# The gated stage of a one-core decoder kernel: another order of loads, four banks for turned rows, and a tile of their own for the narrow unit's weights

## The chip, the cores and the metric

The kernel runs on one core of a Trainium2 chip. The metric is the device time of one execution in microseconds. A core has TensorE (PE, products; PEld is its weight load), VectorE (DVE), ScalarE (ACT), GpSimd (POOL), and SyncE (SP), which in this kernel issues nearly all DMAs. Each engine runs its own list of instructions in order and waits on semaphores.

## The reference

Two gated cross-attention layers and two gated feed-forward layers act on x (16 batches of 128 tokens of 1024 features). The change lies in the last of them, a SwiGLU with low-rank additions to its weights:

```python
def _matmul_lora(x, w, a, b, scale=1.0):
    out = jnp.einsum('bsd,hd->bsh', x, w)
    out = out + jnp.einsum('bsr,hr->bsh', jnp.einsum('bsd,rd->bsr', x, a), b) * scale
    return out
gate = _matmul_lora(x, gate_w, gate_a, gate_b)      # hidden size 2752, rank 16
up = _matmul_lora(x, up_w, up_a, up_b)
hidden = jax.nn.silu(gate) * up
out = _matmul_lora(hidden, down_w, down_a, down_b)
# in the model, with x normalised along its last axis:
x = x + jnp.tanh(g_ffn[1]) * _L1_ffn_ref(_layernorm(x, axis=-1), ...)
```

## The kernel before

The stage before this one (`lane_attention`) normalises its results and stores them in DRAM as x3n, in seven forms of 512 columns for each token (halves and sums of halves). The gated stage (`swiglu_ffn`) computes gate and up for 128 hidden units at a time by a seven-product scheme on 2x2 blocks, in place of eight products. There are 22 such units of weights (NF), the last with 64 hidden columns (`narrow`), and two passes over them, one for each half of the tokens: NU = 44 units in all, LAST = 21. Each product is three matmuls (high and low parts) for each of four column blocks.

**Turned rows.** The token operand of each of the seven products needs four "rows" (128 tokens x 512 columns of x3n), so 28 rows for each pass. SyncE loads a row into one of five places (`row`, L1980: two halves of the third weight tile raw[2], two of lb, one of its own), TensorE turns it into a PSUM bank (`turn`, L2704, counted by xt), ScalarE casts the high part (`high_x`, xh), VectorE subtracts for the low part (`low_x`, xl). Rows 0 to 27 are turned while unit 0's products run, four during each product, one ahead of each column block (`three`, L2747). Rows 28 to 47 are turned during the narrow unit 21, rows 48 to 55 during the first two products of unit 22, which starts the second pass. `turned(n)` says which bank a row is turned into; a turn waits until the row two before it is evacuated. The wait `x_there` at the head of a product lets it start only when all rows of its operand are in place.

**Weights.** In the first pass the raw weights of a unit (gate and up, 512 KB each) are loaded into raw[0] and raw[1] (unit 1: into `second`). TensorE forms their low-rank addition from small factors (`merge`), VectorE adds it in place (`add`, wa), forms four sums (`first_sums`, `second_sums`), ScalarE casts high parts (`high`, `high_sum`, wh), GpSimd subtracts for low parts (`low`, wl). The merged weights are stored in DRAM (`store_merged`) and loaded from there in the second pass. `load_raw(u)` waits until the previous contents are used up (wl) and stored (mst). The narrow unit's 64 + 64 columns are loaded into raw[0].

**Orders.** SyncE's list is written out by hand (L2155 to L2250), and so are ScalarE's (L2391 on) and VectorE's (L2614 on). VectorE's order in one unit is first_and_sixth, gate_even, add, with_seventh, add, first_sums, with_fifth, second_sums, up_even, hidden_even, gate_odd, hidden_odd. The last token row of the first half isn't normalised before the stage begins: VectorE takes its statistics (`last_statistics`), GpSimd the power -0.5, VectorE the normalised row (`last_row`, yn), GpSimd four forms (`row_sums`, tr), and SyncE stores them to x3n. Eight PSUM banks: six go round among the products (`bank`), 6 and 7 serve merges.

## Time and profile before

| | us |
|---|---|
| median of 3 runs | 3319.41 (3316.63 to 3323.08) |
| profiled execution | 3314.45 |
| its span | 3312.5 |
| mean granted clock of TensorE | 0.974 |

The span runs from the first to the last instruction of the one profiled execution. The gated stage begins near 1855 us; its first pass ends and its second begins at about 2340 us; the second ends at 2809 us, followed by the down product. In a timeline, L2715 are turns, L2753 the seven-product matmuls, L2727 merges; "g_ps<-g_ident,h_lb" is a turn of a row that lay in lb, "fe_rows" one in raw[2], "g_xr" one in the fifth place.

### The profile page before, as it was taken

To read this page: it belongs to the slowest core of one execution; us is meant where nothing else is said; L and a number is where in the kernel's file an instruction comes from. 1 tells how busy PE (TensorE), PEld (TensorE's weight loads), DVE (VectorE), ACT (ScalarE), POOL (GpSimd) and SP (SyncE) were. 2 spreads that over 40 slices of the span, in tenths; PEclk is the share of its full clock that TensorE was granted. 3 is DMA by queue.
4 is the path that set the end of the run, shared out by engine and by line. 5 is a ranking of instruction groups with operands and counts; after the bars stand their busy time and mean duration, and the time that the engine had idled before them with its cause. 6 is when DMAs were issued, how large, how long until landed. Compare 5 with 4: busy or idle time off the path is not lost. (4 is left out here: it accounts for less than half of the span.)

```text
span 3312.5 us, 51997 instructions
## 1 busy us (share of the span) xinstructions
PE 3114.8 (94%) x20493; PEld 2369.8 (72%) x20493; DVE 1855.0 (56%) x2538; ACT 1054.5 (32%) x1555; POOL 709.1 (21%) x589
## 2 busy tenths in 40 slices
PE   7999979988599989999999699999899999999999
PEld 6788855555277775666666578887788888777877
DVE  3111138877788838777777478887566665200000
ACT  2222233322233326445554233333433333200000
POOL 0000020000000013333333245554344443000000
PEclk9999989999799999999999899999999999999999
DMA  5334346775522132222222544444544545643343
GB/s 188 118 114 138 122 143 142 156 168 114 210 74 77 64 119 83 78 95 90 106 85 95 164 151 155 155 155 154 159 154 167 171 161 196 221 156 112 126 144 101
DMA packets 370423, 445.61 MB, mean 135 GB/s; under 512 B 157488, under 2 KB 264624, under 8 KB 367296
## 3 DMA queue, kind: packets, MB, share of 16 engines
q1 hardware_dynamic: 354048, 394.04, 37.8%
q10 hardware_dynamic: 16192, 49.04, 4.0%
q8 instruction: 126, 2.06, 0.3%
q14 instruction: 57, 0.47, 0.0%
HBM read 257.69 MB, written 176.79 MB: 131 GB/s over the span
## 5 line engine op out<-in xcount | busy, mean ns | idle before, releaser
L2753 PE MATMUL g_ps<-g_xs,g_wq 128*128 128x512 f32 x2616 | 633.9, 396 | 0.0
L2753 PEld LDWEIGHTS g_ps<-g_xs,g_wq 128*128 128x128 f32 x2616 | 491.3, 190 | 100.7
L2837 PE MATMUL g_ps<-g_wd,g_h 128*128 128x512 f32 x1536 | 354.2, 391 | 0.0
L2837 PEld LDWEIGHTS g_ps<-g_wd,g_h 128*128 128x128 f32 x1536 | 289.9, 189 | 61.9 <-issue 0.9
L2261 POOL TENSOR_TENSOR g_wq<-g_s,g_wq 128x512 fp32r<-128x512 f32 x168 | 242.3, 1453 | 211.6 <-ACT g_wq L2327 211.6
L2261 POOL TENSOR_TENSOR g_wq<-fe_wt,g_wq 128x512 fp32r<-128x512 f32 x127 | 184.6, 1454 | 249.1 <-ACT g_wq L2323 249.1
L2693 DVE TENSOR_TENSOR g_ta<-g_ps,g_ta 128x1024 f32<-128x1024 f32 x4 | 4.9, 1224 | 374.7 <-PE g_ps L2834 374.7
L1369 PE MATMUL kv_gps<-kv_xh,kv_wh 128*128 128x512 f32 x512 | 205.2, 401 | 1.0 <-DVE kv_xl L1266 1.0
L1369 PE MATMUL kv_gps<-kv_xh,kv_wl 128*128 128x512 f32 x512 | 200.3, 391 | 0.0
L1369 PE MATMUL kv_gps<-kv_xl,kv_wh 128*128 128x512 f32 x512 | 200.2, 391 | 0.0
L1665 ACT COPY a_pt<-a_tps 128x1024 f32<-128x1024 f32 x128 | 129.6, 1013 | 205.7 <-PE a_tps L1821 205.5
L946 PE MATMUL f_gps<-f_xt,f_qwh 128*128 128x256 f32 x1024 | 193.4, 290 | 1.4 <-DVE f_xt L841 1.4
L1821 PEld LDWEIGHTS a_tps<-a_ident,a_e 128*128 128x128 f32 x1024 | 110.3, 141 | 98.5 <-issue 83.3
L2327 ACT CAST g_wq<-g_s 128x512 fp32r<-128x512 f32 x168 | 100.3, 620 | 227.1 <-DVE g_s L2517 142.0
L946 PEld LDWEIGHTS f_gps<-f_xt,f_qwh 128*128 128x128 f32 x1024 | 161.2, 193 | 3.7 <-DVE f_xt L841 1.6
L1769 DVE TENSOR_TENSOR a_e<-a_ring,a_mx 128x1024 f32<-128x1024 f32 x128 | 156.7, 1224 | 7.6
L1684 ACT ACTIVATE a_e<-a_e 128x1024 f32<-128x1024 f32 x128 | 135.5, 1059 | 73.7 <-DVE a_e L1769 73.7
L1765 DVE TENSOR_REDUCE a_mx<-a_ring 128x8 f32<-128x1024 f32 x128 | 155.6, 1215 | 0.1
L946 PE MATMUL f_gps<-f_xt,f_qwl 128*128 128x256 f32 x512 | 145.4, 284 | 0.0
L2323 ACT CAST g_wq<-fe_wt 128x512 fp32r<-128x512 f32 x127 | 78.4, 617 | 205.1 <-DVE fe_wt L2498 138.9
L1821 PE MATMUL a_tps<-a_ident,a_e 128*128 128x128 f32 x1024 | 140.7, 281 | 1.6 <-ACT a_pt L1665 1.6
L2753 PE MATMUL g_ps<-h_b,g_wq 128*128 128x512 f32 x528 | 129.5, 393 | 0.8 <-DVE h_b L2483 0.8
(312 smaller groups left out, 5584.4 us busy)
## 6 DMA issues: line engine op xcount, KB each, us to landing
g_h<-g_hidden SPq DMA_DIRECT2D x176, 256.0 KB, 2.7
g_hidden<-g_h ACTq DMA_DIRECT2D x84, 512.0 KB, 3.6
fe_wt<-g_merged SPq DMA_DIRECT2D x43, 512.0 KB, 4.4
g_merged<-fe_wt SPq DMA_DIRECT2D x41, 512.0 KB, 3.6
kv<-kv_y SPq DMA_DIRECT2D x16, 1024.0 KB, 6.4
early_x<-x SPq DMA_DIRECT2D x32, 512.0 KB, 6.1
g_down<-fe_rows SPq DMA_DIRECT2D x22, 512.0 KB, 6.3
fe_wt<-g_down SPq DMA_DIRECT2D x22, 512.0 KB, 4.0
```

The lines of the kernel that those rows point to most:

```text
L946: m = pe.matmul(gps[:, n % 2, 0:2 * P], l[:, n, k, :], xt[c % 2][:, p, k, :], start=(k == 0 and j == 0), stop=(k == NK - 1 and j == 2))
L1369: m = pe.matmul(gps[:, c, :], l[i][:, k, :], r[:, k, 512 * c:512 * c + 512], start=(k == 0 and a == 0), stop=(k == NK - 1 and a == 2))
L1665: act.copy(pt[:, c % 2, :, :], tps[:, :, :]).then_inc(S["te"], 1)
L1684: act.activation(e[:, c % 4, :, :], e[:, c % 4, :, :], ACT.Exp, scale=SCALE).then_inc(S["ex"], 1)
L1765: dve.tensor_reduce(mx[:, c % 2, :], ring[:, sl, :, :], AX.X, ALU.max).then_inc(S["mx"], 1)
L1769: dve.tensor_tensor(e[:, c % 4, :, :], ring[:, sl, :, :], mx[:, c % 2, :].unsqueeze(2).to_broadcast([P, U, P]), ALU.subtract).then_inc(S[" ...
L1821: m = pe.transpose(tps[:, u, :], e[:, c % 4, u, :], ident[:, :])
L2261: pool.tensor_tensor(wq[q % NQ][:, 1, :], src, wq[q % NQ][:, 0, :], ALU.subtract).then_inc(S["wl"], 1)
L2323: act.copy(place_free(q), raw_of(u, m)[:, 512 * a:512 * a + 512]).then_inc(S["wh"], 1)
L2327: act.copy(place_free(quarters(u) + k), sums[i][:, :]).then_inc(S["wh"], 1)
L2753: w = pe.matmul(ps[:, bank(u, to), :], wq[q % NQ][:, l, P * k:P * k + P], xs[j][:, r, k, :], start=(first and k == 0 and a == 0), stop=(la ...
L2837: w = pe.matmul(to, tile[:, p % RING, l, cols], wd[f][:, r, os], start=(f == 0 and a == 0), stop=False)
```

## The change

- The identity for turning is the one that `lane_attention` has made (`last["ident"]`), so the stage's own and the semaphore c1 go.
- VectorE takes the last row's statistics first, `last_row` follows row 7's subtraction; GpSimd takes the power first and does `row_sums` ahead of unit 0's fifth low part.
- `turned(n)`: four banks in turn for rows 0 to 11 and 22 to 49, with the waits in `turn` to match.
- SyncE: row 13 ahead of the wait for the normalised row, rows 14 to 21 ahead of unit 2's weights, rows 22 to 25 ahead of unit 1's store, rows 48 to 51 ahead of unit 23's weights.
- The narrow unit's weights are loaded into raw[2] in the loop at unit 3, with rows 28, 29 and 32 behind them. Rows 30 and 31 (the halves of raw[2]) wait for the narrow unit's last low part and store. Unit 22's weights then wait only for unit 20, and their four sums are formed in unit 20.
- ScalarE's wait for the stores of the last row moves behind two casts.

```diff
@@ -1441,3 +1441,3 @@
         g = early["g"]
-        ident = s.sb("ident", [P, P])
+        ident = last["ident"]
         um1 = s.sb("um1", [P, 2, 16, M])
@@ -1905,3 +1905,4 @@
             "tr": late[:, 1:3, :].rearrange("p a (b n) -> p (a b) n", n=512),
-            "st": s.sb("st", [P, 2, 6]), "mv": s.sb("mv", [P, 2]), "half": s.sb("half", [P, 1]), "rstd": s.sb("rstd", [P, 1])}
+            "st": s.sb("st", [P, 2, 6]), "mv": s.sb("mv", [P, 2]), "half": s.sb("half", [P, 1]), "rstd": s.sb("rstd", [P, 1]),
+            "ident": s.sb("ident", [P, P])}
     tiles = {"raw": [wide[:, 0:D], wide[:, D:2 * D], ffn["rows"][:, 1, :]],
@@ -1976,3 +1977,3 @@
         xr = s.sb("xr", [P, 512])
-        ident = s.sb("ident", [P, P])
+        ident = last["ident"]
         g = s.sb("g", [P, 2])
@@ -1991,3 +1992,3 @@
 
-        names = ("consts down_b c1 gate zl zb xt xh xl sdl wp wa mst sum wh wl m m1 u2 c11 u3 u4 c22 c21 c12 sga sgb "
+        names = ("consts down_b gate zl zb xt xh xl sdl wp wa mst sum wh wl m m1 u2 c11 u3 u4 c22 c21 c12 sga sgb "
                  "hf hh hl dwp dwa dst wh2 wl2 pd res").split()
@@ -2030,4 +2031,4 @@
 
-            if m == 0:
-                return 16 * (u + 1) if u < LAST else 16 * (u + 2)
+            if u == LAST:
+                return 32
             return 16 * (u + 1) if u < LAST else 16 * u
@@ -2037,2 +2038,5 @@
 
+        def down_loaded(d):
+            return 32 + down_added(d)
+
         def batch(q, t):
@@ -2049,3 +2053,5 @@
 
-            return ps[:, (6 if n >= 28 else 4 if n < 16 else 0) + n % 2, :]
+            if n < 28:
+                return ps[:, 2 + n % 4 if n < 12 else 4 + n % 2 if n < 16 else n % 2 if n < 22 else n % 4, :]
+            return ps[:, (6, 7, 1, 2)[n % 4] if n < 50 else 6 + n % 2, :]
 
@@ -2053,3 +2059,7 @@
 
-            return second[m] if u == 1 else raw[m]
+            return second[m] if u == 1 else raw[2] if u == LAST else raw[m]
+
+        def raw_sem(u, m):
+
+            return wld[2] if u == LAST else wld[m]
 
@@ -2069,2 +2079,5 @@
                     sp.wait_ge(S["xt"], n - NROW + 1)
+                if n in (30, 31):
+                    sp.wait_ge(S["wl"], quarters(NF))
+                    sp.wait_ge(S["mst"], 32 * LAST + 16)
                 sp.dma_start(row[n % NROW], rows_in[4 * (n // 28) + t][:, j, :]).then_inc(rl[n % NROW], 16)
@@ -2102,5 +2115,7 @@
                         sp.wait_ge(wld[m], 32)
-                if u > 1:
-                    sp.wait_ge(S["wl"], quarters(u) if u > 2 else quarters(1))
-                    sp.wait_ge(S["mst"], 32 * LAST + 16 if u > LAST else 32 * u if u > 2 else 32)
+                if u == LAST:
+                    sp.wait_ge(S["xt"], 28)
+                elif u > 1:
+                    sp.wait_ge(S["wl"], quarters(LAST) if u == NF else quarters(u) if u > 2 else quarters(1))
+                    sp.wait_ge(S["mst"], 32 * LAST + 16 if u > NF else 32 * min(u, LAST) if u > 2 else 32)
                 if u > LAST:
@@ -2112,3 +2127,3 @@
                     if narrow(u):
-                        sp.dma_start(pieces(raw[0])[:, :, REST * m:REST * m + REST], w[:, :, HID - REST:HID]).then_inc(wld[0], 16)
+                        sp.dma_start(pieces(raw[2])[:, :, REST * m:REST * m + REST], w[:, :, HID - REST:HID]).then_inc(wld[2], 16)
                     else:
@@ -2162,3 +2177,3 @@
             store_merged(0)
-            for n in range(9, 13):
+            for n in range(9, 14):
                 load_row(n)
@@ -2166,4 +2181,3 @@
             sp.dma_start(rows_in[B // 2 - 1, :, 2, :], last["yn1"][:, 512:D]).then_inc(G["out"], 16)
-            load_raw(2)
-            for n in range(13, 17):
+            for n in range(14, 18):
                 load_row(n)
@@ -2171,7 +2185,10 @@
             sp.dma_start(rows_in[B // 2 - 1, :, 3:7, :], last["tr"]).then_inc(G["out"], 16)
+            for n in range(18, 22):
+                load_row(n)
             load_factors(2)
-            for n in range(17, 22):
+            load_raw(2)
+            for n in range(22, 26):
                 load_row(n)
             store_merged(1)
-            for n in range(22, 28):
+            for n in range(26, 28):
                 load_row(n)
@@ -2180,5 +2197,2 @@
                 load_down_factor(d)
-            sp.wait_ge(G["out"], 48)
-            for n in range(28, 33):
-                load_row(n)
             for u in range(1, LAST):
@@ -2186,10 +2200,15 @@
                     load_factors(u + 3)
-                store_merged(u + 1)
-                load_raw(u + 2)
-            for n in range(33, 40):
-                load_row(n)
-            for n in range(40, 48):
+                if u == 3:
+                    load_raw(LAST)
+                    sp.wait_ge(G["out"], 48)
+                    for n in (28, 29, 32):
+                        load_row(n)
+                if u + 1 < LAST:
+                    store_merged(u + 1)
+                    load_raw(u + 2 if u + 2 < LAST else NF)
+            store_merged(LAST)
+            for n in (30, 31, *range(33, 52)):
                 load_row(n)
             load_raw(NF + 1)
-            for n in range(48, 56):
+            for n in range(52, 56):
                 load_row(n)
@@ -2253,7 +2272,2 @@
         def _(pool):
-            pool.memset(ident[:, :], 0.0).then_inc(S["c1"], 1)
-            pool.wait_ge(S["c1"], 1)
-            pool.affine_select(out=ident[:, :], in_=ident[:, :], compare_op=ALU.not_equal, fill=1.0, base=0,
-                               pattern=[[-1, P]], channel_multiplier=1).then_inc(S["c1"], 1)
-
             def low(q, src):
@@ -2273,2 +2287,4 @@
 
+            pool.wait_ge(G["aggr"], 2)
+            pool.tensor_tensor(last["rstd"][:, :], last["mv"][:, 1:2], last["half"][:, :], ALU.pow).then_inc(G["rstd"], 1)
             for u in range(NU):
@@ -2283,4 +2299,3 @@
                     if u == 0:
-                        pool.wait_ge(G["aggr"], 2)
-                        pool.tensor_tensor(last["rstd"][:, :], last["mv"][:, 1:2], last["half"][:, :], ALU.pow).then_inc(G["rstd"], 1)
+                        row_sums()
                     low(q + 4, sums[0][:, :])
@@ -2288,4 +2303,2 @@
                     low(q + 6, sums[3][:, :])
-                if u == 0:
-                    row_sums()
                 if u == LAST - 2:
@@ -2406,5 +2419,5 @@
             silu_even(0)
-            act.wait_ge(G["out"], 48)
             high(1, 0, 0, 0, 1)
             high_sum(1, 1, 1)
+            act.wait_ge(G["out"], 48)
             high_x(20, 21, 22, 23)
@@ -2491,3 +2504,3 @@
                 for m in range(1 if narrow(u) else 2):
-                    dve.wait_ge(wld[m], raw_loaded(u, m))
+                    dve.wait_ge(raw_sem(u, m), raw_loaded(u, m))
                     half = raw_of(u, m)[:, 512 * a:512 * a + 512]
@@ -2527,3 +2540,3 @@
             def add_down(d):
-                dve.wait_ge(wld[2], down_added(d))
+                dve.wait_ge(wld[2], down_loaded(d))
                 dve.wait_ge(S["dwp"], d + 1)
@@ -2603,3 +2616,3 @@
                     dve.bn_stats(st[:, c, :], last["y"][:, 512 * c:512 * c + 512]).then_inc(G["stats"], 1)
-                wait_apart(dve, S["c1"], (G["stats"], 2))
+                dve.wait_ge(G["stats"], 2)
                 dve.bn_aggr(mv[:, :], st[:, :, :]).then_inc(G["aggr"], 1)
@@ -2613,2 +2626,3 @@
 
+            last_statistics()
             add(0, 0)
@@ -2619,6 +2633,5 @@
             low_x(4, 5, 6, 7)
-            last_statistics()
+            last_row()
             low_x(8, 9, 10, 11)
             first_and_sixth(0)
-            last_row()
             low_x(12, 13, 14, 15)
@@ -2643,6 +2656,4 @@
                     low_hidden(u - 1, 0)
-                    low_hidden(u - 1, 1)
-                    first_sums(u + 1)
                     low_x(32, 33, 34, 35)
-                    second_sums(u + 1)
+                    low_hidden(u - 1, 1)
                     low_x(36, 37, 38, 39)
@@ -2655,2 +2666,3 @@
                     low_x(48, 49, 50, 51)
+                    low_x(52, 53, 54, 55)
                 low_hidden(u - 1, 0)
@@ -2666,4 +2678,2 @@
                     continue
-                if u == NF:
-                    low_x(52, 53, 54, 55)
                 first_and_sixth(u)
@@ -2673,7 +2683,8 @@
                 add(u + 1, 1)
-                if not narrow(u + 1):
-                    first_sums(u + 1)
+                after = NF if u + 1 == LAST else u + 1
+                if after < NU - 1:
+                    first_sums(after)
                 with_fifth(u)
-                if not narrow(u + 1):
-                    second_sums(u + 1)
+                if after < NU - 1:
+                    second_sums(after)
                 if u > NF:
@@ -2701,14 +2712,12 @@
         def _(pe):
-            pe.wait_ge(S["c1"], 2)
-
             def turn(n):
                 pe.wait_ge(rl[n % NROW], 16 * (n // NROW) + 16)
-                if n % 28 >= 2:
-                    pe.wait_ge(S["xl"], n - 1)
-                elif n >= 28:
+                if n in (16, 17, 22, 23):
+                    pe.wait_ge(S[{16: "m1", 17: "u2", 22: "c11", 23: "u3"}[n]], 1)
+                elif n in (28, 29):
                     pe.wait_ge(S["wa"], added(LAST) + 2)
-                if n == 16:
-                    pe.wait_ge(S["m1"], 1)
-                elif n == 17:
-                    pe.wait_ge(S["u2"], 1)
+                elif n in (30, 31):
+                    pe.wait_ge(S["c21" if n == 30 else "c12"], full(LAST - 1) + 1)
+                elif n >= 4:
+                    pe.wait_ge(S["xl"], n - 1 if 12 <= n < 22 or n >= 50 else n - 3)
                 for k in range(KH):
```

## Rows read from the trace of the kernel before

**Rows 1.** The page's busy shares; the chain that ended last, one unit.

```profile
PE 3114.8 (94%) x20493; PEld 2369.8 (72%) x20493; DVE 1855.0 (56%) x2538; ACT 1054.5 (32%) x1555; POOL 709.1 (21%) x589
...
2471.47 19.25 PE g_ps L2753 x84
```

**Rows 2.** Windows: length, busy us by engine, clock, DMA share, GB/s.

```profile
1855.14:1923.14 68.00, 43.97 (x213) 34.57 (x213) 39.00 (x56) 25.92 (x46) 24.29 (x21) 0.82 0.63 204
2340.71:2386.60 45.89, 37.48 (x198) 29.87 (x197) 28.12 (x39) 23.55 (x42) 10.03 (x8) 0.89 0.56 178
```

**Rows 3.** TensorE's timeline, start of stage: start, us, what, [idle before <-releaser].

```profile
1855.84 0.74 PE L2727 MATMUL g_ps<-h_sl,h_la 128*128 128x256 f32 x4 [2.95 <-POOL g_ident L2256]
...
1865.68 1.09 PE L2715 MATMUL g_ps<-g_ident,g_xr 128*128 128x128 f32 x4 [1.45 <-DVE g_xs L2483]
...
1867.84 1.05 PE L2715 MATMUL g_ps<-g_ident,fe_rows 128*128 128x128 f32 x4
...
1874.96 0.60 PE L2715 MATMUL g_ps<-g_ident,g_xr 128*128 128x128 f32 x4
...
1876.12 0.63 PE L2715 MATMUL g_ps<-g_ident,fe_rows 128*128 128x128 f32 x4
...
1879.33 0.63 PE L2715 MATMUL g_ps<-g_ident,h_lb 128*128 128x128 f32 x4 [0.75 <-issue]
...
1890.03 1.12 PE L2715 MATMUL g_ps<-g_ident,h_lb 128*128 128x128 f32 x4 [9.37 <-DMA h_lb<-x3n]
...
1896.81 0.63 PE L2715 MATMUL g_ps<-g_ident,fe_rows 128*128 128x128 f32 x4 [0.27 <-issue]
...
1902.46 0.63 PE L2715 MATMUL g_ps<-g_ident,fe_rows 128*128 128x128 f32 x4 [0.28 <-issue]
...
1908.71 1.06 PE L2715 MATMUL g_ps<-g_ident,h_lb 128*128 128x128 f32 x4 [3.79 <-DMA h_lb<-x3n]
...
1913.35 0.63 PE L2715 MATMUL g_ps<-g_ident,g_xr 128*128 128x128 f32 x4 [0.53 <-issue]
...
1920.31 2.99 PE L2753 MATMUL g_ps<-h_b,g_wq 128*128 128x512 f32 x12 [0.80 <-DVE h_b L2483]
```

**Rows 4.** The same view at the boundary between the passes.

```profile
2340.71 0.60 PE L2715 MATMUL g_ps<-g_ident,h_lb 128*128 128x128 f32 x4
...
2351.29 0.63 PE L2715 MATMUL g_ps<-g_ident,g_xr 128*128 128x128 f32 x4 [2.75 <-DVE g_xs L2483]
...
2373.94 1.09 PE L2715 MATMUL g_ps<-g_ident,h_lb 128*128 128x128 f32 x4 [3.22 <-DMA h_lb<-x3n]
...
2385.44 0.60 PE L2715 MATMUL g_ps<-g_ident,fe_rows 128*128 128x128 f32 x4
```

**Rows 5.** A window of 2 us after the stop at 2351.29.

```profile
2354.00:2356.00 2.00, 2.00 (x8) 1.67 (x7) 1.97 (x3) 1.59 (x3) 0.95 (x1) 0.51 0.73 240
```

**Rows 6.** Groups by line, 1855 to 1925: busy us, mean ns | idle before.

```profile
L2483 DVE TENSOR_TENSOR g_xs<-g_ps,g_xs 128x512 fp32r<-128x512 f32 x20 | 13.7, 688 | 19.0 <-ACT g_xs L2309 18.8
...
L2522 DVE TENSOR_TENSOR g_s<-fe_wt 128x512 f32<-128x512 f32 x1 | 1.8, 1769 | 0.0
...
L2309 ACT CAST g_xs<-g_ps 128x512 fp32r<-128x512 f32 x20 | 11.6, 586 | 28.3 <-PE g_ps L2715 28.3
...
L2269 POOL TENSOR_TENSOR h_late<-h_late 128x512 f32<-128x512 f32 x1 | 1.3, 1262 | 0.1
```

**Rows 7.** Issues in the timeline; last row: DMA view, 1850 to 1925, landing.

```profile
1884.48 1.27 SPq L2070 DMA_DIRECT2D h_lb<-x3n  x1
...
2323.34 0.38 SPq L2113 DMA_DIRECT2D fe_wt<-in_L_ffn_gate_w_dram  x1
...
2368.93 0.43 SPq L2070 DMA_DIRECT2D h_lb<-x3n  x1
...
fe_rows<-x3n SPq DMA_DIRECT2D x12, 256.0 KB, 4.0
```

**Rows 8.** TensorE's timeline in unit 19, the merge of unit 20.

```profile
2308.81 1.19 PE L2727 MATMUL g_ps<-h_sl,h_la 128*128 128x256 f32 x4 [4.85 <-DVE fe_wt L2498]
```

2 lines of the change are left out of this document (1 added, 1 removed).

## The prediction

> **What bounds the kernel now.** The profiled execution took 3314.45 us, 1.95 us of it outside its span of 3312.5; the median of the runs shown is 3319.41, 4.96 us more. I sum against the profiled execution and carry the difference over to the median. Read the page's busy shares first: TensorE is busy 94% of the span; then the chain that ended last, where a regular unit of the second pass is one line, 84 products with nothing between [rows 1]. No other engine can shorten such a unit, so a change of order can only act where TensorE isn't in that rhythm. The windows show two such stretches [rows 2]: the start of the gated stage (1855.14 to 1923.14, 43.97 us of products in 68.00 us, granted clock 0.82) and the boundary between its two passes (2340.71 to 2386.60, 37.48 us in 45.89 us, clock 0.89). In both, rows are turned while products run. TensorE's own timeline gives the stops: 2.95, 1.45, 0.75, 9.37, 3.79 and 0.80 us in the start [rows 3], 2.75 and 3.22 us in the boundary [rows 4]. Part of the loss isn't idle time: a row with its three products takes 1.16 us at full clock (1874.96 to 1876.12) but 2.16 us after a stop (1865.68 to 1867.84) [rows 3]; the clock granted after the boundary's first stop was 0.51 [rows 5], the 1.2 GHz level.
>
> **The start, part by part.** I follow the order of each engine in the new code with the durations of [rows 6]. An item of VectorE on a 128x512 tile counts 0.69 us, a cast of ScalarE 0.59.
>
> (a) The mask for turning comes from the stage before, so TensorE's first merge needn't wait for GpSimd's two instructions (released at 1855.84) and can start at 1855.2. VectorE, though, now does the last row's statistics first, 1.8 us by the size of its four items. Then two adds 1.3, a merge 0.8, two adds 1.3, two sums 1.4 and, since rows 2 and 3 have banks of their own, only the subtractions of rows 0 to 3 (2.6) before the first product: 1855.2 + 9.2 = 1864.4, say 1864.6, against 1865.68 [rows 3]. Gain 1.1 us.
>
> (b) Rows 4 to 11 keep their rhythm. The normalisation of the last row goes to where the statistics stood, before row 8's subtraction. The stop of 0.75 us before row 12 (1879.33) stays, and so do its likes: a product needs the last row turned during the one before it, through ScalarE and VectorE, and no bank helps. Gain 0; row 12 is turned at about 1878.2.
>
> (c) Rows 12 to 15. Row 13's load was issued at 1884.48, behind the wait for the normalised row and two 512 KB weight loads, and landed after 5.55 us [rows 3, 7]; TensorE stood 9.37 us for it. It now goes out when row 8 is turned (about 1873.3), and with the usual landing of 4.0 us [rows 7] it is early. Four rows and a merge need 4 x 1.16 + 0.6 = 5.3 us where 17.5 us went (1879.33 to 1896.81), since the three rows at half clock go as well: gain 12.2 us, row 16 at 1883.5. SyncE's new wait, ahead of the loads of rows 18 to 21, is for GpSimd's four row sums. They can start once the normalised row is there (about 1873.8) and GpSimd's fourth low part is done, and take 4 x 1.26 us: 1879.6. Row 17 goes out only at 1878.7, so the wait costs those loads about 0. Behind the sums on GpSimd stands the fifth low part, whose product isn't due before 1889.
>
> (d) Rows 16 to 19: 5.65 us before and after (1896.81 to 1902.46).
>
> (e) Rows 20 to 23 took 10.9 us (1902.46 to 1913.35), 3.79 of them because row 22 stood behind the store of unit 1's weights. What is late next is not a load. ScalarE casts a sum of unit 1 before it takes row 20, so after the second merge (about 1888.9) comes: two adds 1.3, one item 0.7, two sums 0.7 + 1.7, cast 0.6, four casts of rows 2.2, the last subtraction 0.7 = 7.9 us, 1896.8. Four banks let TensorE turn all four rows meanwhile. From row 20 at 1889.2 that is 7.7 us: gain 3.2.
>
> (f) Rows 24 to 27 in the same way: 1.4 + 0.7 + 0.6 + 2.2 + 0.7 = 5.6 us against 6.96: gain 1.3. The seventh product starts at 1902.5 instead of 1920.31.
>
> Sum 1.1 + 12.2 + 3.2 + 1.3 = 17.8 us. Against it stand loads with thin margins, each behind a large transfer: row 18 behind the 1 MB of row sums (issued 1880, needed 1885.9) and row 22 behind unit 2's weights (1886.3, needed 1891.4). A row issued so landed in 5.55 and 5.01 us [rows 3, 4, 7], which is just their need. I take off 1.5 us: 16.3. Bounds: 18 with no stop, 8 with two stops of the 3.79 us kind.
>
> **The boundary.** From row 28 to the end of row 55's products lie 28 rows in 45.9 us; at 1.16 each they need 32.5. The rest went to VectorE, which did two low parts of hidden values and two weight sums between the rows' subtractions with two banks only (2.75 us at 2351.29), to row 48, whose load stood behind unit 23's weights (3.22 us), and to half clock after both [rows 4, 5]. In the new order the four sums of unit 22 are done in unit 20, 2.8 us of VectorE work. They fit where the same steps fit in every other unit, if the weights are there: their load now waits only for unit 20's last low part, when the narrow unit's load was issued before (2323.34 [rows 7]), lands by 2329.3, and the sums are due at 2333.4. Should it slip, VectorE stands in front of unit 20's own results and TensorE behind it, us for us. The narrow unit's weights lie in the third tile since unit 3, issued where SyncE otherwise waits for GpSimd. Rows 30 and 31 share that tile, go out at 2336.2, and are due at 2343. The stores of unit 20's hidden values now hold ScalarE for about 2.2 us, because VectorE's second low part comes after row 35; four banks absorb it (row 40 needs row 36's bank just as it comes free). Unit 23's weights go out at about 2362.5, row 52 at 2363.3; it lands at 2368.3 and is due at 2368.1. So 13.4 less 1.2 for such near misses: 12.2 us. Bounds 6 (one stop of the 3.22 kind with its half clock stays) and 14.
>
> **What costs nothing.** The loads added at unit 3 (1.25 MB) move work out of the start and the end of the pass, where it was waited for. One stop isn't touched: unit 20's merge is 4.85 us late at 2308.81 [rows 8], because SyncE waits for the narrow unit's factor tile to be cleared before it loads unit 20's weights. The new code has the same order there. The second pass is as it was.
>
> Total 16.3 + 12.2 = 28.5 us: 3314.45 - 28.5 = 3286.0 for an execution like the profiled one, 3319.41 - 28.5 = 3290.9 for the median. I forecast **3291**.
>
> **The rivals.**
> - *Late rows remain.* Row loads still stand behind the row sums and the weights of units 2 and 23. If two of the three come 2 us late, each stop costs 2 us and some three rows at 2.16 instead of 1.16, 5 us in all: 28.5 - 10 = 18.5, 3301. For it: the margins above are under 1 us. Against: the issues themselves came late before, here they come as the tile falls free. The Trainium skill (DMA: Bandwidth & Descriptors, "Queues, rings and completion order") says that each DMA engine consumes the descriptors of one queue in ring order, so that a load waits out a large one ahead of it. Row 13 with its 5.55 us agrees.
> - *The clock stays low (the slower side).* With short stops at every product in place of a few long ones, TensorE might never return to 2.4 GHz in these stretches. Then each row takes 2.16 us: 24 rows from 1864.6 with 5 us of stops and merges end at 1921.4, no gain, and the boundary takes 28 x 2.16 = 60.5 instead of 45.9, +14.6: 3334. It decides once some 29 rows more than I reckon run at half clock. Against: stops of 0.75 us didn't bring the clock down (rows at 1.16 on both sides of them), one of 2.75 did [rows 3 to 5]. The Trainium skill (TensorE: Matmul & The Clock Gate, "A second HAM failure mode: psum-queue depth-cycling") tells of a kernel that cycled through its banks and idled briefly so often that the clock swung between its two levels. That is this rival; by it the time would be the 3334 above.
> - *No difference (within 0.2%).* VectorE becomes the bound of both stretches. The same kind of item took it 1769 ns beside a busy GpSimd, instead of 690 [rows 6]; if some 12 of its items there lose 1.1 us each, 13 us go, and with two late rows (10 us) the rest: 3314.
>
> **How the numbers follow.** Forecast 0.62 (3285 to 3297), late rows 0.25 (3297 to 3308), no difference 0.05, low clock 0.04, better than the bounds 0.04. A measurement of this kernel can tell 0.2%, 6.6 us, from no change. Faster 0.91, same 0.05, slower 0.04. The range from 3284 to 3304 leaves out about a third of the late rows, the two last cases and most of the better one: two in ten.
>
> **What would show it.** In the new profile: the first product at about 1864.6; no stop over 1 us at row 13; the row sums' store issued near 1880, ahead of unit 2's weights; rows 20 to 23 turned without a stop and one of about 2.5 us before row 24, by VectorE; the seventh product between 1902 and 1905; 32 to 34 us for rows 28 to 55 at clock 1.00; unit 20's merge still 4.8 us late. It is wrong if TensorE waits over 2 us for a row's load anywhere, if half clock covers more than the first four rows, or if VectorE waits for unit 22's weights in unit 20.

## The result and the profile after

| | before | after |
|---|---|---|
| median | 3319.61 us (3316.63 to 3323.08, 4 runs) | 3290.05 us (3286.94 to 3297.62, 4 runs) |
| ratio, 95% interval | | 0.991 (0.9893 to 0.9928) |
| profiled execution, its span | 3314.45, 3312.5 | 3291.82, 3290.1 |
| mean granted clock of TensorE | 0.974 | 0.976 |

The forecast was 3291 for the median. The page's busy shares, as in [rows 1], show the same work in less time:

```profile
PE 3107.4 (94%) x20493; PEld 2362.6 (72%) x20493; DVE 1852.3 (56%) x2538; ACT 1053.5 (32%) x1555; POOL 708.2 (22%) x587
```

Some 7 of the 22.4 us that the span lost are busy time of TensorE, 3114.8 before: the same instructions, fewer of them at half clock. The windows of the two stretches, to be set beside [rows 2] (length, busy us by engine, clock, DMA share, GB/s):

```profile
1857.31:1906.37 49.06, 36.92 (x211) 29.50 (x212) 36.96 (x56) 25.61 (x46) 22.73 (x18) 0.97 0.77 256
2324.33:2358.41 34.08, 31.83 (x195) 26.17 (x194) 21.77 (x33) 22.65 (x41) 8.98 (x7) 1.00 0.73 239
```

The clock was 0.82 and 0.89 there and is 0.97 and 1.00. TensorE's timeline of the start, to be set beside [rows 3] (start, us, what, [idle before <-releaser]; L2724 are turns, L2762 the seven products' matmuls, L2736 merges). The first product begins with the turn of row 4 (1866.98); the stops of 0.75 us stand before rows 8 and 12 (1874.05, 1879.53):

```profile
1858.05 0.71 PE L2736 MATMUL g_ps<-h_sl,h_la 128*128 128x256 f32 x4 [2.44 <-PEq L1422]
...
1866.98 0.66 PE L2724 MATMUL g_ps<-h_ident,g_xr 128*128 128x128 f32 x4 [4.40 <-DVE g_xs L2496]
...
1868.71 1.05 PE L2724 MATMUL g_ps<-h_ident,fe_rows 128*128 128x128 f32 x4
...
1870.85 0.61 PE L2724 MATMUL g_ps<-h_ident,fe_rows 128*128 128x128 f32 x4
...
1879.53 0.63 PE L2724 MATMUL g_ps<-h_ident,h_lb 128*128 128x128 f32 x4 [0.76 <-issue]
1879.92 0.94 PE L2762 MATMUL g_ps<-g_xs,g_wq 128*128 128x512 f32 x3
1880.69 0.60 PE L2724 MATMUL g_ps<-h_ident,h_lb 128*128 128x128 f32 x4
...
1885.02 0.63 PE L2724 MATMUL g_ps<-h_ident,fe_rows 128*128 128x128 f32 x4 [0.29 <-POOL g_wq L2275]
...
1890.67 0.63 PE L2724 MATMUL g_ps<-h_ident,fe_rows 128*128 128x128 f32 x4 [0.28 <-issue]
...
1894.83 0.66 PE L2724 MATMUL g_ps<-h_ident,h_lb 128*128 128x128 f32 x4 [1.70 <-DMA h_lb<-x3n]
...
1898.39 0.63 PE L2724 MATMUL g_ps<-h_ident,g_xr 128*128 128x128 f32 x4 [1.08 <-issue]
...
1903.93 2.98 PE L2762 MATMUL g_ps<-h_b,g_wq 128*128 128x512 f32 x12 [0.79 <-DVE h_b L2496]
```

Row 13 (1880.69) no longer waits, where TensorE stood 9.37 us. Rows at half clock (1868.71 to 1870.85, 2.14 us) are only the first few; from 1872.00 on the granted clock is 1.00:

```profile
1872.00:1906.37 34.37, 28.72 (x167) 22.66 (x166) 25.73 (x38) 20.14 (x37) 18.37 (x14) 1.00 0.71 237
```

Behind the first product two stops over 1 us remain: 1.70 us before row 22, for its load, and 1.08 before row 24. The boundary, to be set beside [rows 4]:

```profile
2324.33 0.60 PE L2724 MATMUL g_ps<-h_ident,h_lb 128*128 128x128 f32 x4
...
2350.10 0.63 PE L2724 MATMUL g_ps<-h_ident,fe_rows 128*128 128x128 f32 x4 [0.44 <-DVE g_xs L2496]
...
2354.37 0.63 PE L2724 MATMUL g_ps<-h_ident,h_lb 128*128 128x128 f32 x4 [1.81 <-DMA h_lb<-x3n]
...
2357.81 0.60 PE L2724 MATMUL g_ps<-h_ident,fe_rows 128*128 128x128 f32 x4
```

One stop over 1 us, before row 52, is left. Unit 20's merge waits as in [rows 8]:

```profile
2293.38 1.19 PE L2736 MATMUL g_ps<-h_sl,h_la 128*128 128x256 f32 x4 [5.14 <-DVE fe_wt L2511]
```

**Three lengths for all kernels.** Totals of one kernel spread by some 10 us, more than most of the differences below. So I read from TensorE's timeline, for each kernel: L, from the end of the last product of the stage before (the start of the first merge less its stop) to the start of the seventh product; P, from there to row 28; R, from row 28 to row 55. Before, L = 1920.31 - 1855.84 + 2.95 = 67.42, P = 420.40, R = 2385.44 - 2340.71 = 44.73. After, L = 1903.93 - 1858.05 + 2.44 = 48.32, P = 420.40, R = 33.48. That is 19.10 + 11.25 = 30.35 us. The span lost 22.4: the last product of the stage before ended 2.72 us later (1855.61 against 1852.89), and the time from row 55 to the end was 932.29 against 927.06, 5.23 more. In the runs below that end varies from 1853.58 to 1860.72 and that last time from 924.9 to 935.9, also between kernels that don't differ there, so I take both as scatter, which isn't shown further. The medians, over more runs, are 29.6 us apart.

### The profile page after: what moved, and what is told of

It is laid out like the page before. It is cut to its first block and busy times, and to the rows that moved or that the text cites. A ratio compares the mean times of both kernels' runs of the same rounds, so it can differ in the third digit from the quotient of the medians.

```text
span 3290.1 us, 51992 instructions
## 1 busy us (share of the span) xinstructions
PE 3107.4 (94%) x20493; PEld 2362.6 (72%) x20493; DVE 1852.3 (56%) x2538; ACT 1053.5 (32%) x1555; POOL 708.2 (22%) x587
## 5 line engine op out<-in xcount | busy, mean ns | idle before, releaser
L2762 PE MATMUL g_ps<-g_xs,g_wq 128*128 128x512 f32 x2616 | 627.3, 393 | 0.0
L2762 PEld LDWEIGHTS g_ps<-g_xs,g_wq 128*128 128x128 f32 x2616 | 487.0, 189 | 99.9
L1821 PEld LDWEIGHTS a_tps<-h_ident,a_e 128*128 128x128 f32 x1024 | 110.4, 142 | 98.6 <-issue 83.4
L1821 PE MATMUL a_tps<-h_ident,a_e 128*128 128x128 f32 x1024 | 140.5, 280 | 1.8 <-ACT a_pt L1665 1.8
L2762 PE MATMUL g_ps<-h_b,g_wq 128*128 128x512 f32 x528 | 129.5, 393 | 0.8 <-DVE h_b L2496 0.8
```

Source lines behind the costliest of these rows:

```text
L1821: m = pe.transpose(tps[:, u, :], e[:, c % 4, u, :], ident[:, :])
L2762: w = pe.matmul(ps[:, bank(u, to), :], wq[q % NQ][:, l, P * k:P * k + P], xs[j][:, r, k, :], start=(first and k == 0 and a == 0), stop=(la ...
```

## The experiments

All are edits of the kernel after. Each length comes from one profiled execution. Medians and ratios to the kernel before (95% interval), then the lengths of the profiled execution:

| run | median us | ratio | L | P | R |
|---|---|---|---|---|---|
| after | 3290.05 | 0.991 (0.9893 to 0.9928) | 48.32 | 420.40 | 33.48 |
| e1_queue | 3307.2 | 0.9963 (0.995 to 0.9976) | 64.72 | 420.04 | 33.72 |
| e2_banks | 3300.26 | 0.9943 (0.9922 to 0.9963) | 55.36 | 419.01 | 37.93 |
| e3_sums | 3290.65 | 0.9908 (0.9881 to 0.9935) | 48.32 | 419.45 | 36.66 |
| e4_row48 | 3296.09 | 0.9931 (0.9904 to 0.9958) | 48.27 | 419.53 | 41.00 |
| e5_rowsums | 3301.35 | 0.9939 (0.9914 to 0.9963) | 56.58 | 421.45 | 32.86 |
| e6_narrow | 3294.24 | 0.9917 (0.9893 to 0.994) | 48.41 | 420.65 | 33.02 |
| i1_factors | 3285.0 | 0.9893 (0.9875 to 0.991) | 48.30 | 412.17 | 32.33 |
| i2_raws | 3290.6 | 0.9906 (0.989 to 0.9923) | 49.71 | 421.37 | 32.91 |
| i3_stats | 3290.05 | 0.9907 (0.989 to 0.9923) | 48.23 | 419.65 | 32.72 |
| i5_best | 3284.14 | 0.9888 (0.9871 to 0.9906) | 45.85 | 414.32 | 32.88 |
| i6_split | 3287.07 | 0.9896 (0.9878 to 0.9913) | 46.07 | 415.97 | 33.51 |
| i7_order | 3290.15 | 0.9904 (0.9883 to 0.9926) | 47.84 | 415.97 | 33.61 |

**SyncE's old order in the start.** Rows 13 to 17 behind unit 2's weights, rows 22 to 25 behind the store of unit 1.

```diff
-            for n in range(9, 14):
+            for n in range(9, 13):
...
-            for n in range(14, 18):
+            load_raw(2)
+            for n in range(13, 17):
...
-            for n in range(18, 22):
-                load_row(n)
             load_factors(2)
-            load_raw(2)
-            for n in range(22, 26):
+            for n in range(17, 22):
                 load_row(n)
             store_merged(1)
-            for n in range(26, 28):
+            for n in range(22, 28):
```

> The changed kernel with SyncE's order of the stage's start as it was (row 13 behind the wait for the normalised row and unit 2's weights, rows 17 on behind the row sums, unit 1's store ahead of row 22); banks, VectorE, GpSimd and the boundary stay new. Theory (the order of the loads bought most of the start): row 13's load can only go out once unit 2's weights have, and these wait for GpSimd's seventh low part, which now also stands behind the row sums (1883.9 or later), so TensorE stops for 9 to 12 us at row 13 and runs some three rows at half clock after it: the seventh product starts 12 to 15 us later than in the changed kernel, total 3302 to 3306. Rival (the four banks bought the start, the order is a detail): under 5 us, at most 3295.

L grew by 16.40 and the median lies at 3307.2, each a little over the theory's figure and far from the rival's. The loss stands in two places of TensorE's timeline:

```profile
1895.33 1.11 PE L2722 MATMUL g_ps<-h_ident,h_lb 128*128 128x128 f32 x4 [10.33 <-DMA h_lb<-x3n]
...
1914.01 1.12 PE L2722 MATMUL g_ps<-h_ident,h_lb 128*128 128x128 f32 x4 [4.62 <-DMA h_lb<-x3n]
```

SyncE's queue in the timeline, around the load of row 13:

```profile
1878.83 0.34 SPq L2181 DMA_DIRECT2D x3n<-h_late  x1
1888.83 0.38 SPq L2130 DMA_DIRECT2D fe_wt<-in_L_ffn_gate_w_dram  x1
1889.25 0.58 SPq L2130 DMA_DIRECT2D fe_wt<-in_L_ffn_up_w_dram  x1
1889.88 1.13 SPq L2083 DMA_DIRECT2D h_lb<-x3n  x1
```

Row 13 stood behind a wait of 10 us for unit 2's place. In the kernel before that wait was 2.46 us (1880.97 to 1883.43), behind a normalised row that was stored later; here GpSimd does the row sums ahead of the low part that SyncE waits for. So 16.40 us is what the old order of loads costs beside the new order of GpSimd. With it the start takes 64.72 us, of 67.42 before: four banks and the new orders of VectorE and GpSimd do little without the new order of loads.

**Two banks.** The old `turned(n)` and the old waits in `turn`; the loads as after.

```diff
-            if n < 28:
-                return ps[:, 2 + n % 4 if n < 12 else 4 + n % 2 if n < 16 else n % 2 if n < 22 else n % 4, :]
-            return ps[:, (6, 7, 1, 2)[n % 4] if n < 50 else 6 + n % 2, :]
+            return ps[:, (6 if n >= 28 else 4 if n < 16 else 0) + n % 2, :]
```

> The changed kernel with two banks for turned rows as before, all orders new. Theory: each use of the banks shows by itself: the first product starts about 3 us later (rows 2 and 3 wait for the first subtraction), row 22 waits for row 20's subtraction and row 24 comes 2 to 3 us later; at the boundary ScalarE's hold by the stores of the hidden values is no longer absorbed, one stop of 1 to 3 us. Total 7 to 10 us slower than the changed kernel, 3297 to 3300. Rival (banks are only a way to permit the order, TensorE waits for loads anyway): within 3 us, 3290 to 3293.

L grew by 7.04 and R by 4.45, the median to 3300.26, at the top of the theory's range. The first product came 1.62 us later (not 3), rows 4 to 7 took 1.02 more at half clock, rows 20 to 23 2.92 more and rows 24 to 27 1.48 more. The turns waited for VectorE's subtractions, then ran at half clock (a turn of 1.09 us); at the boundary a stop by VectorE came back, 1.93 us where it had been 2.75:

```profile
1899.85 1.09 PE L2722 MATMUL g_ps<-h_ident,h_lb 128*128 128x128 f32 x4 [3.51 <-DVE h_t L2494]
...
2345.09 0.63 PE L2722 MATMUL g_ps<-h_ident,h_lb 128*128 128x128 f32 x4 [1.93 <-DVE h_t L2494]
```

So the banks are worth 7.04 + 4.45 = 11.5 us on top of the new order of loads. The parts overlap, though: 16.40 and 7.04 are more together than the 19.10 us that the start gained.

**Row 48 behind unit 23's weights.**

```diff
-            for n in (30, 31, *range(33, 52)):
+            for n in (30, 31, *range(33, 48)):
                 load_row(n)
             load_raw(NF + 1)
-            for n in range(52, 56):
+            for n in range(48, 56):
```

> The changed kernel with unit 23's weights loaded ahead of row 48, as before, instead of row 52. Theory (a row issued behind 1 MB lands 5 to 7 us after its issue, whichever row it is, and the wait of the weights for GpSimd's last low part comes on top for the earlier row): the stop moves from row 52 (1.8 us in the changed kernel) to row 48 and grows to 3 to 5 us, with three rows at half clock after it, net +3 to +6 us, 3293 to 3296. Rival (TensorE has the same slack there, the stop only moves): within 1 us.

R grew by 7.52, more than the theory's 3 to 6; the median (3296.09) is at the top of its range. The timeline and a window (clock 0.50) show the stop of row 48 and its price, three rows of 2.0 to 2.2 us (2352.26 to 2358.52). Row 42's load was late by 1.43 us besides (2340.21), at full clock:

```profile
2352.26 1.09 PE L2724 MATMUL g_ps<-h_ident,h_lb 128*128 128x128 f32 x4 [5.01 <-DMA h_lb<-x3n]
...
2354.42 1.06 PE L2724 MATMUL g_ps<-h_ident,g_xr 128*128 128x128 f32 x4
```

```profile
2352.26:2356.00 3.74, 3.74 (x13) 3.25 (x14) 0.69 (x1) 1.07 (x2) 0.00 (x0) 0.50 0.62 226
```

**Unit 22's sums back at the boundary.** VectorE's order only; the weights still come early.

```diff
                     low_hidden(u - 1, 0)
-                    low_x(32, 33, 34, 35)
                     low_hidden(u - 1, 1)
+                    first_sums(u + 1)
+                    low_x(32, 33, 34, 35)
+                    second_sums(u + 1)
...
-                after = NF if u + 1 == LAST else u + 1
+                after = NU if u + 1 == LAST else u + 1
```

> The changed kernel with VectorE's order at the boundary as before: the four sums of unit 22 and both hidden low parts between the subtractions of rows 28 to 39. Unit 22's weights are still loaded early. Theory (VectorE's 2.8 us there made the 2.75 us stop of before): four banks let TensorE run up to four rows ahead, which takes up about 3.4 us, so 0 to 3 us are lost, 3290 to 3293, and the stop, if any, comes at rows 36 to 40 by VectorE. Rival (moving the sums is what made room, banks don't help): a stop of 2.8 us or more and half clock after it, 5 us or more.

R was 3.18 longer, at the end of the theory's 0 to 3, and no stop over 0.56 us came before row 52. Some half of the 3.18 came by row 51, which was turned 28.45 us after row 28 (2353.78 - 2325.33), 26.94 in the kernel after: VectorE's added work (0.49 at row 36) and a late load (0.56 at row 42). The other half stands behind row 52. Its load was as slow as in the kernel after (issue to turn 2356.95 - 2349.42 = 7.53 us against 2354.37 - 2346.91 = 7.46), but this time the rows behind it ran at half clock, 5.04 us for the last three steps instead of 3.44:

```profile
2356.95 0.84 PE L2726 MATMUL g_ps<-h_ident,h_lb 128*128 128x128 f32 x4 [1.87 <-DMA h_lb<-x3n]
2357.44 1.63 PE L2764 MATMUL g_ps<-g_xs,g_wq 128*128 128x512 f32 x3
```

**The third tile undone as well.** The narrow unit in raw[0] again, unit 22's weights behind it, sums at the boundary; rows 48 to 51 stay ahead of unit 23's weights, and the banks stay four.

```diff
-            return second[m] if u == 1 else raw[2] if u == LAST else raw[m]
+            return second[m] if u == 1 else raw[m]
...
+            for n in range(28, 33):
+                load_row(n)
             for u in range(1, LAST):
...
-            for n in (30, 31, *range(33, 52)):
+            for n in range(33, 52):
```

> The changed kernel with the narrow unit as before: its weights in the first tile, loaded when unit 20 is used up; rows 28 to 32 loaded in the start; unit 22's weights loaded when the narrow unit is stored, and their four sums with both hidden low parts between the subtractions of rows 28 to 39. Four banks and row 48's place stay new. Theory (the third tile only serves to move the sums out of the narrow unit): as with the sums alone put back (row 28 to row 55 36.7 us against 33.5), since the weights land by 2342 us, before the sums: +3 us or a little more there, 3291 to 3294. Rival (the early load is worth something of its own): +6 us or more, a stop for which VectorE waits on the weights.

The expectation missed: R = 33.02, where some 36.7 was expected, and 0.46 less than after. Row 51 was 0.87 us later here (27.81 us after row 28), by VectorE's sums as in e3_sums, but row 52's load took 6.12 us instead of 7.46 (2355.17 - 2349.05), and the rows behind it ran at full clock:

```profile
2355.17 0.63 PE L2710 MATMUL g_ps<-h_ident,h_lb 128*128 128x128 f32 x4 [0.47 <-DMA h_lb<-x3n]
```

Against the runs with tile and early sums in which row 52 had no stop of 1 us (R of e5, i1, i2, i3 and i5: 32.86, 32.33, 32.91, 32.72, 32.88) 33.02 is 0.1 to 0.7 more. So much, by these single executions, the new tile, the loads from unit 3 on and the early sums are worth at this boundary, once there are four banks and row 48 has its place. The tile, one of the three parts of the change that the title names, bought next to nothing here. The median lies 4 us above that of after, with overlapping ranges; in the profile those microseconds stand behind row 55 (935.9 against 932.3), not in P or R.

**The row sums back behind GpSimd's last low part.**

```diff
-                    if u == 0:
-                        row_sums()
                     low(q + 4, sums[0][:, :])
...
                     low(q + 6, sums[3][:, :])
+                    if u == 0:
+                        row_sums()
```

> The changed kernel with GpSimd's four row sums behind unit 0's seventh low part, as before, where the new order has them ahead of the fifth. SyncE still waits for them ahead of row 18. Theory (moving the sums is what makes SyncE's wait free): the sums end about 4 us later, the loads of rows 18 to 21 go out behind them and their 1 MB store, and TensorE stops 3 to 5 us at row 18 with half clock after it: the seventh product 4 to 6 us later, 3294 to 3296. Rival (the wait is hidden by the 5 rows ahead): under 1 us.

L grew by 8.26 and the median came to 3301.35, both beyond the theory's 4 to 6 us and 3294 to 3296. The store of the row sums went out at 1888.73 instead of 1880.94, rows 18 to 21 with it:

```profile
1888.73 0.34 SPq L2185 DMA_DIRECT2D x3n<-h_late  x1
1889.12 0.43 SPq L2083 DMA_DIRECT2D h_lb<-x3n  x1
```

```profile
1894.46 1.11 PE L2724 MATMUL g_ps<-h_ident,h_lb 128*128 128x128 f32 x4 [6.47 <-DMA h_lb<-x3n]
...
1907.18 0.63 PE L2724 MATMUL g_ps<-h_ident,g_xr 128*128 128x128 f32 x4 [3.29 <-DVE h_t L2496]
```

The new order of loads needs GpSimd's order with it. Without it SyncE's new wait costs TensorE 6.47 us at row 18, and half clock for two rows behind it.

**The factors of unit 21 behind unit 20's weights.** The stop that the prediction left where it was.

```diff
             for u in range(1, LAST):
-                if u + 3 <= LAST:
+                if u + 3 < LAST:
                     load_factors(u + 3)
...
                     load_raw(u + 2 if u + 2 < LAST else NF)
+                if u + 3 == LAST:
+                    load_factors(LAST)
```

> The changed kernel with one more move: SyncE loads the narrow unit's factors behind unit 20's weights instead of ahead of them. Theory (the 5 us stop at unit 20's merge comes from SyncE waiting for the cleared factor tile): the stop goes and with it the half clock behind it (12 products took 4.4 us and more instead of 2.9), 6 to 7 us off the changed kernel, 3283 to 3284, and no stop over 1 us in the first pass. Rival (the weights of unit 20 wait for something else, the store of unit 19's): the stop stays above 3 us, under 2 us gained.

P fell by 8.23. Unit 20's weights were issued at 2282.72 (after: 2286.50), and the merge has no stop:

```profile
2289.34 0.71 PE L2738 MATMUL g_ps<-h_sl,h_la 128*128 128x256 f32 x4
2289.89 2.92 PE L2764 MATMUL g_ps<-g_xs,g_wq 128*128 128x512 f32 x12
```

In the kernel after, the product behind the stop of 5.14 us took 4.38 us for the same 12 matmuls:

```profile
2294.37 4.38 PE L2762 MATMUL g_ps<-g_xs,g_wq 128*128 128x512 f32 x12
```

So the stop was worth 5.14 us, and the half clock behind it 0.5 on the merge and 1.5 on this product, 7.1 of the 8.2. The median (3285.0; expected 3283 to 3284) is 5 us below that of after; the intervals of the two ratios overlap, the 8.2 us in P are far outside what P varies by otherwise (419.0 to 421.5 in all kernels with that stop). It is the largest gain that these runs found on top of the change.

**The statistics behind the first four subtractions.** `last_statistics()` moves behind `low_x(0, 1, 2, 3)`, and GpSimd's power behind its first low part.

```diff
-            last_statistics()
             add(0, 0)
...
             low_x(0, 1, 2, 3)
+            last_statistics()
```

> The changed kernel with VectorE's statistics of the last row behind the subtractions of rows 0 to 3 instead of ahead of the first add, and GpSimd's power behind the first low part. Theory (VectorE's chain sets the first product, 9 us from the start of the stage): the first product comes 1.8 us earlier, the seventh too, since the normalised row is still there before the row sums can start: 3288. Rival (the statistics only move, later stops take the gain): the seventh product comes within 0.5 us of where it was.

First merge to first product is 1864.19 - 1856.02 = 8.17 instead of 8.93 us: of the statistics' 1.8 us only 0.76 had stood on the chain, for VectorE would have waited for TensorE's merge anyway, 1.88 us in this run's timeline of VectorE:

```profile
1856.77 1.29 DVE L2512 TENSOR_TENSOR fe_wt<-g_ps,fe_wt 128x512 f32<-128x512 f32 x2 [1.88 <-PE g_ps L2737]
```

And L fell by only 0.09: the theory (1.8 us) missed and the rival held. More of the first rows ran at half clock (the turn 1.09 us, where after had 0.66), so that row 8 came 7.63 us after the first product, not 7.07; that alone took 0.56 of the 0.76 back. TensorE's timeline:

```profile
1864.19 1.09 PE L2725 MATMUL g_ps<-h_ident,g_xr 128*128 128x128 f32 x4 [4.40 <-DVE g_xs L2497]
```

**Both raw loads behind their rows.** Unit 2's weights behind row 27 and unit 23's behind row 55.

```diff
             load_factors(2)
-            load_raw(2)
             for n in range(22, 26):
...
+            load_raw(2)
             load_factors(3)
...
-            for n in (30, 31, *range(33, 52)):
+            for n in (30, 31, *range(33, 56)):
                 load_row(n)
             load_raw(NF + 1)
-            for n in range(52, 56):
-                load_row(n)
```

> The changed kernel with unit 2's weights loaded behind row 27 and unit 23's behind row 55. In the three runs so far with the new order of loads the stop at row 22 (a load, 0.92 to 1.70 us) and the one at row 24 (VectorE, 1.08 to 1.84) add up to 2.78 each time. Theory (VectorE's chain before row 24 is the bound, the late row 22 is inside it): the stop at row 22 goes, the one at row 24 becomes 2.8, nothing gained in the start; at the boundary the stop at row 52 goes, 1.8 us: 3288. Rival (the loads are the bound): both go, 4.6 us, 3285.5.

Both load stops went, as the theory had it, but R fell by 0.57 only (1.8 expected), and L rose by 1.39 (0 expected). The stop of row 22 moved to row 24, where VectorE is late, became one of 3.01 us, and half clock came behind it:

```profile
1896.51 1.09 PE L2722 MATMUL g_ps<-h_ident,g_xr 128*128 128x128 f32 x4 [3.01 <-DVE h_t L2494]
1897.25 1.63 PE L2760 MATMUL g_ps<-h_t,g_wq 128*128 128x512 f32 x3
```

In the kernel after, the load that was late by 1.70 us hid that VectorE was late by 2.78 in all.

**VectorE's and ScalarE's order in unit 0's end**, with the factors of i1_factors: the sums of unit 1 behind the subtractions of rows 20 to 27.

```diff
             with_seventh(0)
-            first_sums(1)
             low_x(20, 21, 22, 23)
             with_fifth(0)
-            second_sums(1)
             low_x(24, 25, 26, 27)
+            first_sums(1)
+            second_sums(1)
```

> The changed kernel with the narrow unit's factors behind unit 20's weights, and in the start rows 20 to 27 ahead of unit 1's sums on ScalarE and VectorE. Unit 2's weights stay ahead of row 22. Theory: 8.2 us from the factors; of the 2.78 us at rows 22 and 24 the part that VectorE caused goes, the late load of row 22 (0.9 to 1.9 us) stays: 9 to 10 us below the changed kernel, 3280 to 3281. No stop of its own in unit 1 or 2. Rival (the sums of unit 1 then come late): a stop of over 1 us in unit 1.

The forecast (3280 to 3281) missed by 9 us; the median is that of after. Row 24's stop fell to 0.75, row 22's load kept 1.49, and L is 0.48 less than after. P is 3.8 more than i1_factors has, with a new stop:

```profile
1921.92 0.71 PE L2738 MATMUL g_ps<-h_sl,h_la 128*128 128x256 f32 x4 [1.78 <-DVE fe_wt L2513]
```

Its cause runs over three engines. GpSimd has no sum of unit 1 to work on until 1907.65 and then does six low parts in a row, to 1915.98 (in the kernel after they are spread and end at 1907.90). ScalarE's first cast of hidden values is written to wait for them (`high_hidden`, wl) and comes at 1916.07 instead of 1907.98, the silu behind it. VectorE waits 6.81 us for that silu, with unit 2's additions in its list behind it. GpSimd's timeline, then VectorE's:

```profile
1907.65 1.64 POOL L2277 TENSOR_TENSOR g_wq<-g_s,g_wq 128x512 fp32r<-128x512 f32 x1 [11.70 <-ACT g_wq L2342]
...
1914.70 1.28 POOL L2277 TENSOR_TENSOR g_wq<-g_s,g_wq 128x512 fp32r<-128x512 f32 x1
```

```profile
1917.25 0.75 DVE L2584 SCALAR_TENSOR_TENSOR g_hf<-g_tc,g_g,g_ta 128x512 f32<-128x512 f32 x1 [6.81 <-ACT g_ta L2366]
```

The other 2.0 us of the 3.8 I haven't placed. The three lengths together are 4.8 us below those of after (497.4 against 502.2), which the medians don't show; that stays open.

**Split loads.** i7_order with unit 2's two weight loads and unit 1's two stores spread between rows 22 to 27.

```diff
-            load_raw(2)
-            for n in range(22, 26):
+            load_raw(2, (0,))
+            for n in range(22, 24):
                 load_row(n)
-            store_merged(1)
-            for n in range(26, 28):
+            load_raw(2, (1,))
+            for n in range(24, 27):
```

> As the kernel before it, with the two large transfers of the start split in halves of 512 KB: unit 2's gate weights ahead of row 22, its up weights ahead of row 24, the first half of unit 1's store ahead of row 27, the second behind it. Theory (a row is late by what stands ahead of it in the queue, 512 KB less is about 1.4 us less): no load stop over 0.5 us in the start, and unit 2's merge isn't late as it was with its weights behind row 27: 10.5 to 11.5 us below the changed kernel, 3278.5 to 3279.5. Rival (splitting spreads the lateness over two rows): same start as the kernel before it within 0.5 us.

In the start the theory held: row 22 has no stop, row 24 one of 0.76, and L is 46.07, 2.25 below after and 1.77 below i7_order. But P has the stop of 1.78 as i7_order has, and the median, 3287.07, is 8 us above the forecast.

**All together.** i1_factors, i2_raws, i3_stats and the order of i7_order.

> All three moves together, and in the start ScalarE and VectorE take rows 20 to 27 before the sums of unit 1 (casts and subtractions of rows 20 to 23, then 24 to 27, then unit 1's sums and their casts). Theory: 7 us (unit 20's merge), 1.8 (row 52), 1.8 (statistics) and 2.8 (VectorE's chain before row 24) add up to 13.4: 3276 to 3278. Rival (one of the gains is taken by a later wait: unit 1's low parts come late for its products, or rows 24 to 27 wait for their loads): a new stop in unit 1, 3280 or more.

The forecast (3276 to 3278) missed and the rival, a new stop in unit 1 and 3280 or more, held. L = 45.85 and P = 414.32. Its three lengths sum to 493.05, i1_factors' to 492.80, after's to 502.20, before's to 532.55. The two medians (3284.14 and 3285.0) can't be told apart. What the loads and orders win in L is lost to the 1.78 us stop and what follows it. i1_factors, one moved load, has nearly all of the gain. By their medians both beat the kernel after by some 5 us, with overlapping intervals of the ratios, and the one before by some 35.

## Why the prediction was right

By its own steps, counted from the end of the last product of the stage before (1852.89 before, 1855.61 after):

| step | predicted | measured | gain predicted, measured |
|---|---|---|---|
| (a) to the first product | 11.71 | 11.37 | 1.1, 1.42 |
| (b), (c) to row 16 | 18.9 | 18.04 | 12.2, 13.09 |
| (d) to row 20 | 5.65 | 5.65 | 0, 0 |
| (e) to row 24 | 7.7 | 7.72 | 3.2, 3.17 |
| (f) to the seventh product | 5.6 | 5.54 | 1.3, 1.42 |
| late loads in the start | | | -1.5, 0 |
| boundary | | | 12.2, 11.25 |
| sum | | | 28.5, 30.35 |

- *(a)* The mechanism held: the wait for GpSimd went and the statistics took its place. The chain from the statistics to the first product was put at 9.2 us and took 9.08 (1857.90 to 1866.98), the statistics 1.7 of it. Their net price is less, since without them VectorE waits for the merge: i3_stats gets back 0.76. That the first product comes 1.42 us earlier all the same is the banks' doing: with two it comes 1.62 later (e2_banks). The prediction named the stop of 1.45 us in the kernel before but not the one of 3.53 before rows 2 and 3 (1862.29), which the banks removed with it (in e2_banks it is back, 3.52 us):

```profile
1862.29 1.94 PE L2715 MATMUL g_ps<-g_ident,h_lb 128*128 128x128 f32 x8 [3.53 <-DVE g_xs L2483]
```

- *(b), (c)* Row 13 in time, SyncE's wait for the row sums at no cost (their store at 1880.94, "near 1880"). That it costs nothing hangs on GpSimd's order, as e5_rowsums shows (6.47 us). The 0.9 us over the forecast come from (b), where the gain was taken as 0: the first product's start to row 8 took 7.07 us (1866.98 to 1874.05) and 8.11 before, where three rows had run at half clock (1.09, 1.05, 1.05 us a turn) and now it is fewer. No step of the sum had that gain; it came unforeseen.
- *(e)* The length is right to 0.02 us and its inside only half. The prediction named VectorE's chain with one stop of about 2.5 us before row 24. Measured were 1.70 for row 22's load and 1.08 at row 24, 2.78 in all. The chain itself shows in ScalarE's and VectorE's timelines: ScalarE waits 2.37 us for a sum of unit 1, then casts four rows, and VectorE waits 1.17 for these.

```profile
1892.99 1.64 DVE L2530 TENSOR_TENSOR g_s<-g_s,g_second 128x512 f32<-128x512 f32 x1
1895.81 2.48 DVE L2496 TENSOR_TENSOR h_t<-g_ps,h_t 128x512 fp32r<-128x512 f32 x4 [1.17 <-ACT h_t L2322]
```

```profile
1894.67 0.62 ACT L2340 CAST g_wq<-g_s 128x512 fp32r<-128x512 f32 x1 [2.37 <-DVE g_s L2530]
1895.19 2.04 ACT L2322 CAST h_t<-g_ps 128x512 fp32r<-128x512 f32 x4
```

i2_raws takes the load away and finds the chain's 3.01 us behind it: the sum of the two stops was set by the chain, so the 1.5 us taken off for late loads in the start were not paid: row 22's delay lay inside a wait that step (e) had already counted, and row 18 wasn't late. In five other kernels with this order (e3, e4, e6, i1, i3) the two stops split differently (0.92 and 1.84, 1.17 and 1.61, 0.97 and 1.79, 1.90 and 0.87, 1.09 and 1.68) and sum to 2.76 to 2.78.
- *The boundary.* Predicted was 33.7 us for 28 rows with the allowance, measured 33.48 to row 55's start and one row more, 34.6. A row took 1.13, not 1.16 us, and row 52 was later than foreseen: 7.46 us from issue to turn, where the prediction used 5.0. Its times held as well, once moved by the 16.38 us by which row 28 now comes earlier (2340.71 - 2324.33): unit 22's weights were issued at 2307.91 (predicted 2323.34 - 16.38 = 2306.96), VectorE took the first sum without a wait for them at 2316.95 (2333.4 - 16.38 = 2317.0), and rows 30 and 31 went out at 2319.77 (2336.2 - 16.38 = 2319.8). VectorE's timeline, then SyncE's:

```profile
2316.95 0.68 DVE L2527 TENSOR_TENSOR g_s<-fe_wt 128x512 f32<-128x512 f32 x1
...
2319.77 0.81 SPq L2083 DMA_DIRECT2D fe_rows<-x3n  x2
```

  The two causes that it named first are real by experiment: banks (4.45, e2_banks) and row 48's place (7.52, e4_row48). The third, VectorE's sums of unit 22 between the rows, is much smaller than its place in the argument: it moves rows by 0.9 us (e6_narrow) to at most 1.5 (e3_sums, with a late load in it), and with row 52 in time R is 0.1 to 0.7 us longer for it. The prediction gave this part no number of its own, so the sum didn't suffer. Whether the median's 4 us more in e6_narrow are scatter stays open.
- *What costs nothing.* Unit 20's stop stayed (5.14 for 4.85), for the reason given: i1_factors moves the wait that stood ahead of the load and the stop is gone.
- *The rivals.* Late rows: two loads did come 1.7 and 1.8 us late, but the first lay in the shade of VectorE, and neither cost clock, so 1.8 of the rival's 10 us were paid. Low clock: a row ran at 1.13 to 1.18 us on both sides of the stops of 0.75 (1879.53) and after 1.70. The Trainium skill (TensorE: Matmul & The Clock Gate, "A second HAM failure mode: psum-queue depth-cycling") tells of a kernel that cycled through banks and idled briefly between its groups so often that the clock swung between its two levels. Here, with four banks, stops of 0.75 us before rows 8 and 12 and of 1.70 and 1.08 later, the granted clock was 1.00 from 1872.00 on, so this trace doesn't show it. VectorE as the bound of both stretches: it set the first product, row 24 and the seventh product, as the sum had it, and at the boundary no stop by it was over 0.44 us. That rival's 1769 ns isn't the price of the 690 ns kind of item: it is a sum that reads both its operands in SBUF, against subtractions of which one operand lies in PSUM. In the kernel after, with GpSimd at work, such sums took 1.48 (1866.79) and 1.64 us (1892.99) and the subtractions 0.69; with GpSimd idle such a sum took 0.69 as well (i7_order, 1906.23).
- *The total.* 30.35 us in the three lengths against 28.5; the medians differ by 29.6. The overshoot in the start (1.3 in the steps, 1.5 for loads) and the shortfall at the boundary (0.95) partly cancel, which makes 3290.05 against 3291 look better than the terms are. The single execution that was profiled took 3291.82 us where the sum gave 3286.0: the 2.72 and 5.23 us outside the three lengths are in it. So a hit within 1 us is in part luck.

## What to carry to other kernels

Look in the in-order queue of the issuing engine for small, urgent loads that stand behind a wait for a large one's place, and move them ahead; but move with them whatever that queue now waits for (e5_rowsums). Before taking away a late load, see which engine is late behind it: its stop may only move, and half clock may come behind it (i2_raws). A stop that looks left over deserves its own experiment: two factor loads behind two weight loads gave 8 us in their stretch, more than the two further banks gave in the start. And test each part of a change by itself: the new tile and the early sums gave 0.1 to 0.7 us at the boundary (e6_narrow).
